# Feed-forward rows of groups 1 to 3 turned by 32x32 squares on VectorE and sixteen SBUF to SBUF transfers, instead of by TensorE

## What is computed

```python
x = x + jnp.tanh(g_xattn[0]) * _L0_xattn_ref(_layernorm(x), ctx_4096, ctx_4096, ...)
x = x + jnp.tanh(g_ffn[0]) * _L0_ffn_ref(_layernorm(x), W_org, lora_down, lora_up, lora_keys, Wq)

def _L0_ffn_ref(x, W_org, lora_down, lora_up, lora_keys, Wq):
    base = jnp.einsum('bsi,oi->bso', x, W_org)
    q = jnp.einsum('bi,ki->bk', x.mean(axis=1), Wq)
    coeffs = jax.nn.softmax(jnp.einsum('bk,ek->be', q, lora_keys) / math.sqrt(K), axis=-1)
    h = jnp.einsum('bsi,eir->bser', x, lora_down)
    return base + jnp.einsum('be,bser,ero->bso', coeffs, h, lora_up)
```

## Time and profile before

| | |
|---|---|
| time, median of 3 | 1332.57 us (1332.13 to 1335.5) |
| the profiled execution | 1335.65 us, its span 1333.8 us |
| mean granted clock of TensorE | 0.997 of full speed |
| busy: TensorE, VectorE, ScalarE, GpSimd | 98%, 54%, 31%, 47% of the span |
| chain that ended last | TensorE 79%, GpSimd 12%, VectorE 3%, DMA 2% |

### The profile page before, as it was taken

One profiled execution on the slowest core, in us unless ns is written; L12 is line 12 of the kernel. 1 busy time (PEld: TensorE's weight loads), 2 busy tenths in 40 slices (PEclk: granted clock), 3 DMA queues, 4 the chain that ended last, 5 costly groups with the idle time before them and its releaser, 6 DMA issues.

```text
span 1333.8 us, 22141 instructions
## 1 busy us (share of the span) xinstructions
PE 1312.6 (98%) x8224; PEld 1103.8 (83%) x8224; DVE 720.7 (54%) x1363; ACT 410.0 (31%) x743; POOL 630.6 (47%) x801
## 2 busy tenths in 40 slices
PE   9999999999989999999999999999999999999999
PEld 8888887888868878787888888888788888888887
DVE  5333343445885566577777777777875243243110
ACT  3322221111112213355655555555451120111100
POOL 0799999999934433456565665655500000000000
PEclk9999999999989999999999999999999999999999
DMA  6898746444469998989888878777443202211011
GB/s 217 245 309 231 209 105 174 173 174 176 153 216 232 255 242 210 291 260 256 232 236 231 235 224 229 224 222 218 171 173 111 79 32 83 76 63 63 32 44 52
DMA packets 195850, 238.65 MB, mean 179 GB/s; under 512 B 29344, under 2 KB 129824, under 8 KB 195744
## 3 DMA queue, kind: packets, MB, share of 16 engines
q1 hardware_dynamic: 162384, 189.12, 46.6%
q10 hardware_dynamic: 33360, 48.13, 13.4%
HBM read 152.23 MB, written 83.90 MB: 177 GB/s over the span
## 4 chain that ended last, share of the span: by engine, by line
PE 79%; POOL 12%; DVE 3%; issue 2%; DMA 2%; ACT 1%; SPq 0%; ACTq 0%; DVEq 0%; POOLq 0%
PE bank L161 16%; PE bank L162 16%; PE bank L163 16%; PE bank L1632 5%; POOL mixed_part L918 5%; PE bank L1652 5%; PE bank L1667 4%; PE bank L1613 4%; PE bank L1614 4%; PE bank L1615 4%; POOL mixed_sum L925 3%; POOL mixed_sum L918 2%; POOL value_in L925 2%; PE bank L1639 1%; PE bank L360 1%
## 5 line engine op out<-in xcount | busy, mean ns | idle before, releaser
L1820 DVE TRANSPOSE_TENSOR_REDUCE part<-bank 128x16 f32<-128x512 f32 x256 | 174.2, 692 | 2.9 <-PE bank L1632 0.5
L1766 ACT ACTIVATE probT<-bank 128x512 f32<-128x512 f32 x256 | 138.9, 595 | 90.1 <-PE bank L1652 86.7
L1440 DVE SCALAR_TENSOR_TENSOR raw_d<-bank,gates,raw_d 128x512 f32<-128x512 f32 x32 | 24.0, 750 | 163.0 <-PE bank L163 163.0
L1613 PE MATMUL bank<-w_hi,oT_hi 128*128 128x512 f32 x256 | 108.1, 422 | 1.2 <-POOL oT_lo L1933 1.2
L161 PE MATMUL bank<-place_a,w_hi 128*128 128x512 f32 x256 | 100.5, 392 | 7.4 <-DVE place_a L154 7.4
L706 DVE SCALAR_TENSOR_TENSOR stage_lo<-bank,bias_mixed,stage_hi 128x512 fp32r<-128x512 f32 x46 | 34.4, 750 | 132.9 <-ACT stage_hi L708 132.9
L161 PE MATMUL bank<-w_hi,yT_hi 128*128 128x512 f32 x256 | 100.9, 394 | 0.0
L161 PE MATMUL bank<-place_b,place_a 128*128 128x512 f32 x256 | 99.7, 390 | 0.9 <-DVE place_c L154 0.9
L1614 PE MATMUL bank<-w_lo,oT_hi 128*128 128x512 f32 x256 | 100.5, 393 | 0.0
L1615 PE MATMUL bank<-w_hi,oT_lo 128*128 128x512 f32 x256 | 100.3, 392 | 0.0
L163 PE MATMUL bank<-place_a,w_lo 128*128 128x512 f32 x256 | 100.1, 391 | 0.0
(11 more groups left out here) (248 smaller groups left out, 3188.5 us busy)
## 6 DMA issues: line engine op xcount, KB each, us to landing
k_rows<-stage_hi SPq DMA_DIRECT2D x128, 128.0 KB, 2.7
v_pad<-v_out SPq DMA_DIRECT2D x32, 512.0 KB, 2.8
v_place<-v_pad ACTq DMA_DIRECT2D x64, 256.0 KB, 4.3
tin<-in_ctx_cols SPq DMA_DIRECT2D x26, 512.0 KB, 4.0
k_in<-k_rows SPq DMA_DIRECT2D x64, 192.0 KB, 3.0
q_in<-q_rows SPq DMA_DIRECT2D x128, 96.0 KB, 3.4
q_rows<-wq_own SPq DMA_DIRECT2D x81, 128.0 KB, 5.2
raw_d<-x_mid SPq DMA_DIRECT2D x17, 512.0 KB, 3.3
```

Of the source, the lines that this page charges most:

```text
L1613: pe.matmul(o_bank[out][:], hi[:, c, :], wo_hi[:, k, cols], start=(k == 0), stop=False)
L1766: act.activation(probT[o % NPT][:, i].rearrange("k a p q -> k (a p q)"), two_bank[i][:], ACT.Exp).then_inc(s_exp, 1)
L1820: dve.tensor_reduce(part[o % NS][:, :, 2 * i:2 * i + 2, :].rearrange("k a p b -> k a (p b)"), one_bank[i][:].rearrange("k (a b t) -> k a b ...
```

## The change

Tiles 4 to 15 are no longer turned by TensorE. After the normalisation VectorE turns the tile in place of its 32x32 squares: `dve.transpose` of the whole 128x1024 tile into a new tile `yturn[slot]` (two of them), each square turned where it stands. Then 16 transfers bring the squares to where a fully turned tile has them, from `yturn` back into `yin`: one for each pair of a band i of 32 source partitions and a band j of 32 target partitions, each of 32 partitions x 8 pieces of 32 numbers (128 bytes). ScalarE issues the eight of i = 0, 1, behind its root in `act_pre`; SyncE issues the eight of i = 2, 3. Both wait for the turned tile. The two turning jobs become `column_jobs`, without TensorE: ScalarE and VectorE now read `yin` in SBUF instead of the bank, and wait until all 16 transfers have landed. They stand behind the tile's first `out_job` (before it for a group's last tile). They keep their numbers in the list of jobs. The load of the next tile into `yin` now waits until these jobs are emptied. The four loads of `lora_up` share one semaphore, and all wait for all four.

```diff
             def y_norm(n, job):
                 b, slot, use = ARRIVAL[n], n % 2, (n - GB) // 2
                 free = t_end[ARRIVAL[n - 2 if use else n - GB]]
 
                 def load(sp):
-                    line.wait_filled(sp, free)
+                    if use:
+                        sp.wait_ge(line.emptied, free)
+                    else:
+                        line.wait_filled(sp, free)
                     sp.dma_start(yin[slot], x_mid[b * P:(b + 1) * P, :]).then_inc(s_yin[slot], 16)
                 plan.append((free - 0.45, load))
-                job.dve_pre = norm.vector_steps(...)
-                job.act_pre = norm.scalar_step(n - GB)
+                def turn_squares(dve):
+                    normalise(dve)
+                    dve.wait_ge(norm.s_done, n - GB + 1)
+                    if use:
+                        dve.wait_ge(s_ycols[slot], y_columns_in(n - 2))
+                    dve.transpose(yturn[slot][:], yin[slot]).then_inc(s_yturn, 1)
+
+                def place_squares(eng, rows):
+                    eng.wait_ge(s_yturn, n - GB + 1)
+                    by_square = yturn[slot][:].rearrange("p (k j t) -> p j k t", j=SQUARES, t=BLOCK)
+                    columns = yin[slot].rearrange("p (k i t) -> p i k t", i=SQUARES, t=BLOCK)
+                    for i in rows:
+                        for j in range(SQUARES):
+                            eng.dma_start(columns[j * BLOCK:(j + 1) * BLOCK, i],
+                                          by_square[i * BLOCK:(i + 1) * BLOCK, j]).then_inc(s_ycols[slot], 16)
+                def root_and_squares(act):
+                    root(act)
+                    place_squares(act, (0, 1))
+                job.dve_pre, job.act_pre = turn_squares, root_and_squares
+                plan.append((line.jobs.index(job) + 0.7, lambda sp: place_squares(sp, (2, 3))))
...
+            def column_jobs(n, read_end):
+                def landed(eng):
+                    eng.wait_ge(s_ycols[n % 2], y_columns_in(n))
+                def free(act):
+                    landed(act)
+                    line.wait_filled(act, read_end)
+                for half in range(2):
...
+                    def empty(bank, cols=cols, part=part, hi=hi, lo=lo):
+                        nc.vector.tensor_reduce(msum[:, part, b % GB:b % GB + 1],
+                                                tile[:, cols].rearrange("p (q s) -> p q s", q=4), AX.X, ALU.add)
+                        return split_lo(lo, tile[:, cols], hi)
+                    t_end[b] = line.add(Job(None, empty, act=lambda bank, cols=cols, hi=hi: split_hi(hi, tile[:, cols]),
+                                            act_wait=free, dve_wait=landed))
...
                     if more and n:
                         y_norm(n + GB, carrier)
-                        y_jobs(n + GB)
+                    read_end = len(line.jobs)
+                    if more and i == GB - 1:
+                        column_jobs(n + GB, read_end)
                     carrier = out_job(n, 0, h_end)
+                    if more and 0 < n and i < GB - 1:
+                        column_jobs(n + GB, read_end)
...
                     if n == 0:
                         y_norm(GB, carrier)
                         carrier = out_job(n, 1, h_end)
-                        y_jobs(GB)
+                        column_jobs(GB, read_end)
```

More of the change, by code:

```diff
@@ L1218, in build @@
             s_arrive = [s_raw_d[1]] + [sem(f"s_arrive{i}") for i in range(1, len(arrive))]
-            s_up = [sem(f"s_up{i}") for i in range(LC)]
+            s_up = sem("s_up")
             s_yin = [sem(f"s_yin{i}") for i in range(2)]
+            s_yturn, s_ycols = sem("s_yturn"), [sem(f"s_ycols{i}") for i in range(2)]
+            yturn = [sb(f"yturn{i}", [P, D], F32, attend) for i in range(2)]
             s_xres = [sem(f"s_xres{i}") for i in range(2)]
@@ L1250, in slot_of @@
                 return b % GB + b // GB % 2
+            BLOCK = 32
+            SQUARES = P // BLOCK
             def y_norm(n, job):
@@ L1257, in load @@
                 def load(sp):
-                    line.wait_filled(sp, free)
+                    if use:
+                        sp.wait_ge(line.emptied, free)
+                    else:
+                        line.wait_filled(sp, free)
                     sp.dma_start(yin[slot], x_mid[b * P:(b + 1) * P, :]).then_inc(s_yin[slot], 16)
                 plan.append((free - 0.45, load))
-                job.dve_pre = norm.vector_steps(n - GB, yin[slot], lambda dve: dve.wait_ge(s_yin[slot], 16 * (use + 1)))
@@ L1262, in y_norm @@
-                job.act_pre = norm.scalar_step(n - GB)
+                normalise = norm.vector_steps(n - GB, yin[slot], lambda dve: dve.wait_ge(s_yin[slot], 16 * (use + 1)))
+                def turn_squares(dve):
[12 more added lines that the diff above has]
+                                          by_square[i * BLOCK:(i + 1) * BLOCK, j]).then_inc(s_ycols[slot], 16)
@@ new lines, in y_norm, with y_columns_in @@
+                root = norm.scalar_step(n - GB)
+                def root_and_squares(act):
[3 more added lines that the diff above has]
+                plan.append((line.jobs.index(job) + 0.7, lambda sp: place_squares(sp, (2, 3))))
+            def y_columns_in(n):
+                return 16 * SQUARES * SQUARES * ((n - GB) // 2 + 1)
+            def column_jobs(n, read_end):
+                b, tile = ARRIVAL[n], yin[n % 2]
+                at = slot_of(b)
+                def landed(eng):
[4 more added lines that the diff above has]
+                for half in range(2):
+                    cols, part = slice(half * HALF, (half + 1) * HALF), slice(4 * half, 4 * half + 4)
+                    hi, lo = (y[:, at, part, :].rearrange("p a b -> p (a b)") for y in (yT_hi, yT_lo))
+                    def empty(bank, cols=cols, part=part, hi=hi, lo=lo):
[4 more added lines that the diff above has]
+                                            act_wait=free, dve_wait=landed))
@@ L1266, in y_jobs, with wait @@
                 at = slot_of(b)
[L1267 to L1278, removed]
+                def wait(pe):
+                    pe.wait_ge(s_fdone, FIRST_ORDER.index(n) + 1)
+                    if n == 2:
+                        pe.wait_ge(s_max, OCTS)
+                    if n == 0:
+                        pe.wait_ge(s_exp, 2 * OCTS)
+                    if n == 1:
+                        pe.wait_ge(s_o, HALVES)
+                tile, sums = first_y[n], msum[:, :, b:b + 1] if n < GB - 1 else None
                 t_end[b] = transpose_jobs(line, tile, wait, yT_hi[:, at, :, :], yT_lo[:, at, :, :], sums=sums)
@@ L1324, in up_chunk @@
                     up_raw[k],
-                    lora_up.rearrange("e r o -> (e r) o")[k * P:(k + 1) * P, :]).then_inc(s_up[k], 16)))
+                    lora_up.rearrange("e r o -> (e r) o")[k * P:(k + 1) * P, :]).then_inc(s_up, 16)))
                 def landed(eng):
-                    eng.wait_ge(s_up[k], 16)
+                    eng.wait_ge(s_up, 16 * LC)
                 def free(act):
```

## The result

| | before | changed kernel |
|---|---|---|
| median, 8 runs each | 1334.41 us (1332.13 to 1336.71) | 1342.54 us (1339.08 to 1347.99) |
| ratio of the times, 95% interval | | 1.0069 (1.005 to 1.0087) |
| the profiled execution, its span | 1335.65, 1333.8 us | 1346.87, 1345.1 us |
| mean granted clock of TensorE | 0.997 | 0.990 |

Slower by 0.7%, against a forecast of no difference; 1342.5 lies 1.5 us above the range. The sign is that of the rival "slower by the issuing", which gave 1340.5.

What follows compares the result with a forecast made beforehand. TensorE, busy for 98% of the span, was taken to bound the kernel: 1335.65 - 10.5 (transposes) + 9.4 (wait) + 1.5 (clock) = 1336.05 us profiled, 1333.0 in the runs' measure, no difference. Range: 1327.5 to 1341 us.

Steps and rivals of the forecast that it cites:

- slower by the issuing: Rival, chance 0.28: the two queues hinder each other, issues cost 0.80 us each, all three groups wait, 1340.5 us.
- Group 0, step by step: Walk through tiles 4 to 7 up to the scores of group 1: TensorE waits 9.4 us there.
- transposes: TensorE is spared 0.875 us a tile, 10.5 us for the twelve tiles 4 to 15.
- later eights: ScalarE's eight square issues for each tile after tile 4 take 5.4 us, 0.67 each.
- load of tile 7 landed: Group 0, load of tile 7 into yin: 3.2 us, from 1034.4 to 1037.6.
- wait of group 1: TensorE ahead of the scores of group 1: tile 7 taken over at 1054.1, wanted at 1044.75, wait 9.4 us.
- h part of group 1: h_lo behind the squares of tile 8 ends at about 1085.25, wanted at 1085.4: just holds, no wait.
- 2.4 to spare, no wait: Groups 1 and 2: at 16.6 us a cycle, tile 11 is taken over at 1134.9, wanted at 1137.3.
- The clock: TensorE after its wait in group 1: granted clock of 0.5 for a while, 1.5 us lost.
- Issuing: Square transfers on ScalarE: 0.67 us per issue, taken from 64x4 transfers by number of pieces and dimensions.
- The rival that let the gain stay: Chance 0.20: issues in a row go out at 0.34 us each, the wait is gone, 1322.1 us.
- The small pieces: Squares land in 3.3 us a tile, hidden behind issuing; rival, chance 0.05: 32 ns a piece, 8.2 us, 1335.0.

Runs made afterwards that it cites:

- all reordered: Changed kernel with tile 6's steps one job later, roots of tiles 5 and 7 amid ScalarE's transfers, groups 1 and 2's first-tile columns before out_job; 1324.76 us, ratio 0.9921.
- wait filled: Changed kernel with 52 matmuls that nobody reads put on TensorE ahead of the scores of group 1; 1342.01 us, ratio 1.0047 to before.
- group 0 by TensorE: Changed kernel with tiles 4 to 7 turned by TensorE as before and only tiles 8 to 15 by squares; 1332.9 us, ratio 0.9988.
- tile 6 hung later: Changed kernel with the steps of tile 6 hung one job later, on the second out_job of tile 1; 1333.64 us, ratio 0.9997.
- early root: Changed kernel with ScalarE's root of tile 5 between the two fours of tile 4's transfers; 1341.94 us, ratio 1.0035.
- group 0 reordered: Changed kernel with tile 6's steps one job later and the roots of tiles 5 and 7 between the fours of ScalarE's transfers; 1329.37 us, ratio 0.9952.
- half the pieces: Changed kernel with ScalarE's transfers carrying four of their eight blocks of columns, 128 pieces instead of 256; 1341.78 us, ratio 1.0049.
- ScalarE silent: Changed kernel with ScalarE placing no squares and SyncE's eight per tile unchanged, half the squares left out; 1329.61 us, ratio 0.9959.

## Why the prediction was wrong

The mechanism was right, in its place and its order; its size was too small, and the two later scores that were called safe were not. In the step "Group 0, step by step", with my times shifted by the 1.9 us of this execution:

| step | forecast | measured |
|---|---|---|
| transposes | -10.5 | -9.9, all reordered, with 0.2 of waits left |
| turning a tile | 1.25 | 1.25 |
| squares of tile 4, ScalarE | 5.4 | 6.80 |
| later eights | 5.4 | 5.52 |
| load of tile 7 landed | 3.2 | 4.0 |
| tile 7 taken over, shifted | 1056.0 | 1059.7 |
| scores wanted, shifted | 1046.6 | 1047.3 |
| wait of group 1 | 9.4 | 12.5 |
| clock behind it | 1.5 | 2.5 |
| waits of groups 2 and 3 | 0 | 1.5, 0.6 |
| clock behind these | 0 | 1.6, 0 |
| h part of group 1 | 0.15 to spare | no wait |

- **The wait of group 1** was mis-sized by 3.1 us: tile 7 was taken over 3.7 later, the scores wanted 0.7 later. Nearly every link of a chain of 55 us was forecast a little short: the first eight by 1.4 us (its last issue alone took 1.78), the other three by 0.1 each, the load of tile 7 by 0.8, and the rest in taking over and in the load of tile 6. For the load of tile 7 I had taken nearly the shortest of landings of 3.1 to 5.8.
- **"2.4 to spare, no wait"** in groups 1 and 2 is the step that failed outright. I had 16.6 us for a cycle; it took 17.8 (from 1110.8, the last issue for tile 9, to 1128.6 for tile 10). Of that 1.2 more, the load is 0.7 (issued at 1114.08, first statistics at 1118.02), taking over 0.3, issuing 0.1. From tile 8 to 9 it was 1.05 longer than said (the eight of tile 9 took 6.31), then 1.2 and 1.4, and 0.25 at the end: 3.9 us, and 2.4 to spare became 1.5 late. A margin counted in cycles has to be held against the error of a cycle times their number.
- **The clock.** I priced it at one wait, by one measured case. After the wait of only 1.48 us it fell too and cost 1.6 us, and behind the long one it cost 2.5.
- **The h part of group 1** did hold, but in the run with the wait filled, where TensorE comes 2.5 us earlier, it waits 1.29 us for `h_lo`.
- **Issuing** was right at 0.67 (0.69), by the number of pieces and dimensions, which was mostly the wrong reason: from 256 pieces to 32 plain rows an eight falls only from 5.52 to 5.03. The rival that let the gain stay rested on 0.34, the price of a transfer of whole rows by itself; a square's takes 0.60 even by itself, so the rival's 0.20 was too much. Of the slower rival the sign was right and the price not: 0.69, and 0.85 for the first eight alone, whose cause was not tried. So the kernel came out on this rival's side, but by the many small links and the clock and not by its price.
- **The small pieces** were no cost: landing took 1.9 us (3.6 at most), and VectorE never waited for squares.
- **The range** had a slip at its lower end: a wait of 5 us without loss of clock is 1332.57 - 10.5 + 5, or 1327.1, not 1327.5. Its upper end, 1341, is the slower rival's 1340.5, which counts one low clock of 1.5 us; there were two, of 4.1 together.
- **The chances** followed one term, the price of an issue. The other links of the same chain had errors too, and every one that was measured lengthened it; "slower" deserved more than 0.28.

## What to carry to other kernels

A transfer issued by a computing engine is an instruction of that engine, and what counts is what stands behind it: the same 192 transfers cost 0.7% (8 us) in one order and save 0.8% (10 us) in another. Before adding issues to an engine, write down its order and ask of each root, copy or load behind them who waits for it, and take the queue's time per issue from a row of several transfers of the same kind, not from a single one of another kind. Where a chain runs through a cycle of buffers, its spare time shrinks with each turn, and a wait that is removed moves the demand of the next one forward.

## What was not expected of the hardware

- An issue of a transfer from SBUF to SBUF of 32 partitions took 0.51 to 0.60 us by itself and 0.61 to 0.64 in a row (medians of single issues), for 32, 128 or 256 pieces and for plain rows. An issue of 128 whole rows took 0.32 to 0.34 by itself, 0.46 each in a pair and 0.60 right behind squares. Eight contiguous transfers cost nearly as much as eight of 256 pieces.
- The length of a short wait of TensorE did not tell what the clock did. Behind waits of 1.48 (changed kernel), 1.44 (wait filled), 2.62 (group 0 by TensorE) and 3.11 us (tile 6 hung later) the granted clock fell to 1.2 GHz. Behind 2.30 (early root) and 2.47 us (group 0 reordered) it stayed at 2.4 GHz, as behind all of 1.3 us and less. It also stayed behind a wait of 1.48 with half the pieces, the same length in the same place as where it fell in the changed kernel:

```profile
1150.00:1154.00 4.00, 3.80 (x31) 3.19 (x32) 1.93 (x7) 0.30 (x2) 0.00 (x0) 1.00 0.51 179
```

- The first eight issues of ScalarE, beside SyncE's sixteen, took 6.80 us instead of 5.52; 1.78 of it is the last issue. With ScalarE silent, SyncE's first sixteen took 11.50 instead of 10.40, so the other queue is not the only cause.
